# A two-layer graph network on one core: the first edge pass over windows of 32 nodes, its rows moved within SBUF

## The chip, the cores and the metric

The kernel runs on one core of one Trainium2 chip. The metric is the device time of one execution in microseconds (us). Before the change the median of three runs is 3838.8 us (3837.41 to 3846.68).

## What is computed

There are N = 3125 nodes with 128 features, E = 100,000 edges with 64 features, and for each edge a source and a destination node; the edges come sorted by destination. The first layer is, with `seg` a softmax or sum over the edges of a destination:

```python
h = node_features @ node_fc_W + node_fc_b
he = edge_features @ edge_fc_W + edge_fc_b
hs, hd = (h[src], h[dst])
a = jnp.sum(hs * hd, axis=-1)
t = jax.nn.relu(jnp.einsum('ed,mdf->emf', he, rel_att_W1) + rel_att_b1[None])
g = jax.nn.sigmoid(jnp.einsum('emf,mf->em', t, rel_att_W2) + rel_att_b2[None])
alpha = _seg_softmax(a, dst, n)
beta = _seg_softmax(g, dst, n)
s_att = jnp.einsum('ed,kdf->ef', hs, node_att_W)
h_att = jax.ops.segment_sum(alpha[:, None] * s_att, dst, num_segments=n) / kk
t_rel = jnp.einsum('ed,mdf->emf', hs, rel_att_W)
msg_rel = jnp.einsum('em,emf->ef', beta, t_rel)
h_rel = jax.ops.segment_sum(msg_rel, dst, num_segments=n) / mm
h_red = jax.nn.relu(jnp.concatenate([h_att, h_rel], axis=-1) @ out_fc_W + out_fc_b)
```

A node without edges keeps h; a gate of the node's features mixes this with the features; a layer norm follows. The second layer takes a softmax over all edges of a score `tanh(q[src] + k[dst]) @ phi`, sums messages by source, and ends in another layer norm.

## The kernel before

The program is five blocks, each with code for the five engines, joined by barriers.

**Block 1** (L327 to L912, to 683.6 us). SP loads the inputs (L330 to L356), TensorE projects the nodes in 25 blocks of BN = 125 (L470 to L486), and SP writes each block to `h_table` (rows) and `hT_table` (transposed) in DRAM (L368 to L373). ScalarE copies results out of the banks. Then comes the edge MLP in 100 "octs" of 8 x 125 edges: TensorE transposes the edge features (L526), makes six hidden products of 500 columns (L536) and six logit products (L547) that each fill 32 rows of a bank; ScalarE applies relu (L667), tanh and exp. Beside it VectorE sorts the edges by source for the second pass and makes both passes' plans: tables that say for each step which group of edges and which block of nodes it treats. At the end VectorE splits the edge weights into bf16 parts (L853 to L857) and SP writes records of ten words for each edge (L378, `rec0`).

**Block 2, the first edge pass** (L916 to L1164, 683.6 to about 2227 us). GROUPS = 196 groups of 512 edges meet NB = 25 blocks of nodes in STEPS = 220 steps; a step treats one group for one block. It is a loop of ten steps (SU); the ring of gathered rows has five slots (RING). In a step:

- SP reads group and block from the plan by two `value_load` (L969, L970) and loads the records (L972) and the block's node vectors `hbT` (L973).
- POOL gathers 4 x 128 rows of `h_table` by indirect DMAs (L984) into `hs`, two steps and more ahead.
- TensorE turns back the exponentials of step n (L1022), turns the rows (L1000) and the one-hot table (L1006) of step n + 2, makes the scores of step n + 1 (L1017), the relation sums (L1030), their weights' sums (L1033) and the attention sums (L1039) of step n.
- ScalarE copies the turned rows (L1061), makes a mask of the turned one-hot (L1063), the exponentials (L1073), and copies them turned back (L1069).
- VectorE makes the one-hot table (L1101, L1104), the maximum over scores and mask (L1126), the weighted one-hot (L1111), and adds the sums to the block's (L1140, L1143, L1145), with a running maximum and a factor `shrink` (L1075) between steps.

The order of work on each engine is written out by hand in the function `body` of each; what an engine may start is set by semaphores. TensorE's order and the slot rule of the gathers are:

```python
turn_back(s, k); turn(*step_of(s, k, 2)); scores(*step_of(s, k, 1)); relations(s, k); attention(s, k)
pool.wait_ge(stepped, s * SU + k + SU - RING + 1)
```

**Block 3** (L1170 to L1404) turns the sums into outputs (L1226 to L1237, L1361), applies gate and layer norm (L1366 to L1378), and writes the tables of keys, values and queries. **Block 4** (L1411 to L1690) is the second edge pass, 220 steps of the same kind, with gathers at L1482 and TensorE's sums at L1528. **Block 5** writes the output.

## Time and profile before

| | |
|---|---|
| median of 3 runs | 3838.8 us (3837.41 to 3846.68) |
| profiled execution | 3869.89 us |
| its span | 3868.0 us, mean granted clock 0.837 |
| TensorE (PE) busy | 2980.1 us (77%) |
| VectorE (DVE) | 2193.4 us (57%) |
| GpSimd (POOL) | 1902.0 us (49%) |
| ScalarE (ACT) | 1479.6 us (38%) |
| DMA | 231,858 packets, 217.93 MB, 161,623 of them under 512 B |

The span runs from the first to the last instruction; the execution's own time is the one to compare with the runs. Busy shares are averages over five blocks with different limits. The granted clock is the TensorE clock that was allowed, as a share of the full 2.4 GHz. PEld is TensorE's loading of weights. In the rows, `arena` is the memory that holds `hs`, the weighted one-hot and, in block 1, the hidden layers.

### The profile page before, as it was taken

The numbers are of one execution on the slowest core, as the hardware profiler recorded it, in microseconds if no ns is written. First come the engines' busy times: TensorE is split into PE (matmuls) and PEld (weight loads), VectorE is DVE, ScalarE is ACT, GpSimd is POOL, SyncE is SP. The second block draws the span as 40 slices with busy tenths as digits, with TensorE's granted clock in tenths as the row PEclk, the third lists the DMA queues.
The fourth block names the chain that finished last, engine by engine and source line by source line (L and its number), as shares of the span: only waits on it lengthen the run. The fifth ranks groups of instructions, "written<-read, shape, count | busy, mean of one in ns | idle before, by whom it ended". The sixth has DMA issues, their size and how long they took to land. (4 is left out here: it accounts for less than half of the span.)

```text
span 3868.0 us, 66746 instructions
## 1 busy us (share of the span) xinstructions
PE 2980.1 (77%) x17025; PEld 2039.3 (53%) x17025; DVE 2193.4 (57%) x5947; ACT 1479.6 (38%) x3759; POOL 1902.0 (49%) x1791
## 2 busy tenths in 40 slices
PE   5999999698989889898889936665665666656663
PEld 3444333466666666666666634554554555545552
DVE  8455210566666656666656673655555555555554
ACT  3777776233333334333333322222222222222221
POOL 0000000566666656666656502666666666666660
PEclk9999999799999989999999965776667777677675
DMA  2111121212212112222212102222222222222220
GB/s 69 57 45 45 55 76 39 60 48 52 52 49 50 50 47 52 49 52 51 49 48 50 39 2 60 72 70 70 70 71 72 70 70 71 71 71 72 71 69 19
DMA packets 231858, 217.93 MB, mean 56 GB/s; under 512 B 161623, under 2 KB 190124, under 8 KB 231787
## 3 DMA queue, kind: packets, MB, share of 16 engines
q0 software_dynamic: 70400, 144.29, 14.0%
q1 hardware_dynamic: 161387, 72.74, 7.5%
q8 instruction: 38, 0.62, 0.1%
q14 instruction: 33, 0.27, 0.0%
HBM read 203.65 MB, written 13.22 MB: 56 GB/s over the span
## 5 line engine op out<-in xcount | busy, mean ns | idle before, releaser
L984 POOL DMA_INDIRECT arena<-h_table,rec x880 | 976.4, 1110 | 545.8 <-issue 249.9
L1482 POOL DMA_INDIRECT arena<-kv_table,rec_sb x880 | 911.8, 1036 | 471.7 <-issue 235.3
L1030 PE MATMUL bank<-arena 128*128 128x375 f32 x1760 | 611.3, 490 | 0.0
L1528 PE MATMUL bank<-arena,probT 128*125 128x193 f32 x1760 | 513.8, 456 | 122.3 <-DVE probT L1646 65.6
L1528 PEld LDWEIGHTS bank<-arena,probT 128*125 128x125 f32 x1760 | 422.8, 265 | 179.7 <-DVE probT L1646 103.3
L1030 PEld LDWEIGHTS bank<-arena 128*128 128x128 f32 x1760 | 349.4, 199 | 302.0 <-issue 122.6
L1522 PE MATMUL bank<-top_run,ones 1*128 1x1 f32 x440 | 108.6, 313 | 367.8 <-DVE top_run L1625 196.4
L1111 DVE TENSOR_TENSOR arena<-onehot,rec 128x1500 f32<-128x1500 bf16 x220 | 376.5, 1711 | 0.0
L536 PE MATMUL bank<-eaT,wc 64*128 64x500 f32 x1200 | 360.8, 616 | 0.0
L1572 ACT COPY hotT<-bank 125x512 bf16<-125x512 bf16 x220 | 128.1, 582 | 580.4 <-remote 514.3
L1126 DVE CUSTOM_DVE_ANT_0 score<-bank,mask,m_old 125x512 f32<-125x512 f32 x220 | 165.2, 751 | 296.3 <-remote 178.8
L1522 PEld LDWEIGHTS bank<-top_run,ones 1*128 1x128 f32 x440 | 89.9, 253 | 453.2 <-DVE top_run L1625 243.1
L667 ACT ACTIVATE arena<-bank,bias 128x500 f32<-128x500 f32 x534 | 314.6, 684 | 36.6 <-PE bank L536 32.3
L977 POOL MEMSET arena<- 128x20 f32 x1 | 0.1, 134 | 649.5 <-POOLq L328 649.5
L1069 ACT COPY probT<-bank 128x500 f32<-128x500 f32 x220 | 126.8, 576 | 439.3 <-PE bank L1022 309.4
L1073 ACT ACTIVATE prob<-score,m_neg 125x512 f32<-125x512 f32 x220 | 158.8, 722 | 343.4 <-DVE m_neg L1129 308.6
L1022 PE MATMUL bank<-identf,prob 125*128 125x125 f32 x880 | 146.5, 292 | 165.5 <-issue 95.2
L1017 PE MATMUL bank<-hsT,hbT 128*125 128x512 f32 x440 | 272.0, 704 | 0.0
L1039 PE MATMUL bank<-arena,probT 128*125 128x129 f32 x1760 | 248.6, 283 | 0.0
L1617 DVE TENSOR_TENSOR arena<-bank,arena 128x256 f32<-128x256 f32 x220 | 92.7, 421 | 245.3 <-remote 235.9
L536 PEld LDWEIGHTS bank<-eaT,wc 64*128 64x128 f32 x1200 | 133.1, 186 | 164.1 <-ACT arena L667 105.9
L1646 DVE TENSOR_TENSOR probT<-onehot,p_e 128x500 f32<-128x500 bf16 x220 | 149.7, 680 | 115.9 <-ACT p_e L1565 80.1
(291 smaller groups left out, 4881.7 us busy)
## 6 DMA issues: line engine op xcount, KB each, us to landing
ea<-in_edge_attr SPq DMA_DIRECT2D x100, 250.0 KB
arena<-h_table,rec POOLq DMA_INDIRECT x880
arena<-kv_table,rec_sb POOLq DMA_INDIRECT x880
hbT<-hT_table SPq DMA_DIRECT2D x220, 62.5 KB
qb<-q_table SPq DMA_DIRECT2D x220, 46.9 KB
rec<-rec SPq DMA_DIRECT2D x220, 20.0 KB
rec<-rel_st SPq DMA_DIRECT2D x5, 781.2 KB
rec_sb<-rec SPq DMA_DIRECT2D x220, 4.0 KB
```

What stands on the lines that cost most here:

```text
L536: pe.matmul(bank[1 + (6 * o + n) % 4][:, 0:4 * LANES], wc[half * DE:(half + 1) * DE, m * D:(m + 1) * D], eaT[half * DE:(half + 1) * DE, o ...
L667: act.activation(hid[o % 3 * 6 + n], bank[1 + (6 * o + n) % 4][:, 0:4 * LANES], ACT.Relu, bias=bias1[:, m:m + 1]).then_inc(hid_sb, 1)
L984: pool.indirect_dma_start(out=hs[:, k % RING, j, 0:D], out_offset=None, in_=h_table, in_offset=bass.IndirectOffsetOnAxis(ap=rec_v[:, k, j, ...
L1017: pe.matmul(bank[2][0:BN, :], hbT[:, k, :], hsT[:, k % 2, :], start=True, stop=True).then_inc(score_ps, 1)
L1030: pe.matmul(bank[6 + k % 2][:, 0:M * BN], hs[:, k % RING, j, 0:D], hot_w_v[:, k % 2, j, :], start=(j == 0), stop=(j == GT - 1))
L1039: last = pe.matmul(bank[4 + k % 2][0:BN, 0:D + 1], probT_v[:, k % 2, j, :], hs[:, k % RING, j, :], start=(j == 0), stop=(j == GT - 1))
L1073: act.activation(prob[:, k % 2, :], score[:, k % 2, :], ACT.Exp, bias=m_neg[:, k % 2:k % 2 + 1]).then_inc(prob_done, 1)
L1111: v.tensor_tensor(hot_w[:, k % 2, :].rearrange("p (j m n) -> p j m n", j=GT, m=M), onehot_v[:, k % RING, :, :].unsqueeze(2).to_broadcast([ ...
L1126: v.tensor_tensor_reduce(score[:, q, :], bank[2][0:BN, :], mask[:, q, :], 1.0, m_old[:, q:q + 1], ALU.add, ALU.max, m_new[:, q:q + 1]).the ...
L1482: pool.indirect_dma_start(out=row_v[:, k % RING, j, 0:KV], out_offset=None, in_=kv_table, in_offset=bass.IndirectOffsetOnAxis(ap=rec_v[:, ...
L1522: pe.matmul(bank[3][:, 0:1], ones[0:1, :], top[0:1, k:k + 1], start=True, stop=True).then_inc(top_ps, 1)
L1528: last = pe.matmul(bank[4 + k % 2][0:BN, 0:KV + 1], probT_v[:, k % 2, j, :], row_v[:, k % RING, j, AD:RK], start=(j == 0), stop=(j == GT - 1))
```

## The change

- Node blocks have 128 rows for 125; the last has 53.
- The first pass goes over windows of WN = 32 nodes: 98 windows, STEPS0 = 296 steps in a loop of eight. Each of the four sub-groups of 128 edges of a step sums into its own 32 rows of a bank, so the accumulators `att_acc` and `rel_acc` hold four partial sums (of lanes) that block 3 merges. The sums of weights come from a column of ones in `hs`.
- POOL gathers once for each group (196 x 4 gathers, written out without a loop) into a landing ring of four groups in `y_sb`. For each step SP moves the group's 4 x 128 rows from there into a second ring `hs` of four slots by a DMA within SBUF, and reads three numbers from the plan. VectorE reads four and ScalarE one.
- The records of the first pass go: source, destination and weight stay in SBUF by group (`src_g`, `dst_g`, `w_g`). `src_g` and `dst_g` are loaded again from the inputs in pieces of 16 B, and all tables of nodes must have been written before ScalarE starts on the edge MLP.
- The MLP has 98 octs of 8 x 128 edges. The bf16 split of the weights goes, and the counting that makes the plan runs over 98 windows.
- Block 3 has a merge of the lanes' maxima and sums, a rescaling of the accumulators in five pieces, and tables written without a ring. Blocks 4 and 5 change only in size.

The diff, cut to its core:

```diff
-BN = 125
-NB = N // BN
+BN = 128
+NB = -(-N // BN)
+NP = NB * BN
+LAST = N - (NB - 1) * BN
...
+WN = 32
+WINS = -(-N // WN)
...
+STEPS0 = -(-(GROUPS + WINS - 1) // SU0) * SU0
+SH = 4
+RING0 = 4
...
-                    with sp.Fori(0, NB // W) as s:
-                        for k in range(W):
-                            b = s * W + k
-                            sp.wait_ge(hT_sb, b + 1)
-                            sp.dma_start(h_table[bass.ds(b * BN, BN), :], hblk[:, k, :]).then_inc(h_out[k], 16)
-                            sp.dma_start(hT_table[bass.ds(b, 1), :, :].rearrange("o d n -> (o d) n"), hT[:, k, :]).then_inc(h_out[k], 16)
...
+                        def load_group(table, name):
+                            sp.dma_start(table[:, 0:COLS - GT].rearrange("p (g j) -> p g j", j=GT),
+                                         i[name][0:FULL].rearrange("(g p j) -> p g j", p=128, j=GT)).then_inc(groups_in, 16)
+                            sp.dma_start(table[0:TAIL, COLS - GT:],
+                                         i[name][FULL:].rearrange("(p j) -> p j", j=GT)).then_inc(groups_in, 16)
+
+                        for o in range(U):
+                            load_edges(o)
+                        load_group(dst_g, "dst")
+                        load_group(src_g, "src")
+                        for b in range(NB):
+                            sp.wait_ge(hT_sb, b + 1)
+                            sp.dma_start(h_table[b * BN:(b + 1) * BN, :], h_sb[:, b, :]).then_inc(h_out, 16)
+                            sp.dma_start(hT_table[:, b * BN:(b + 1) * BN], hT[:, b, :]).then_inc(h_out, 16)
+                        for o in range(U, OCTS):
...
+                    act.wait_ge(h_out, 32 * NB)
...
                 def _(sp):
-                    with sp.Fori(0, STEPS // SU) as s:
-                        for k in range(SU):
-                            n = s * SU + k
-                            g = sp.value_load(plan_row[0][0:1, bass.ds(n * 2, 1)], min_val=0, max_val=GROUPS - 1)
-                            b = sp.value_load(plan_row[0][0:1, bass.ds(n * 2 + 1, 1)], min_val=0, max_val=NB - 1)
-                            sp.wait_ge(stepped, n + 1)
-                            sp.dma_start(rec[:, k, :], rec0_v[bass.ds(g, 1), :, :].rearrange("o p w -> (o p) w")).then_inc(loaded[k], 16)
-                            sp.dma_start(hbT[:, k, :], hT_table[bass.ds(b, 1), :, :].rearrange("o d n -> (o d) n")).then_inc(loaded[k], 16)
+                    sp.wait_ge(cleared_a, 1)
+                    sp.sem_inc(moved[SH - 1], 16)
+                    with sp.Fori(0, STEPS0 // SU0) as s:
+                        for k in range(SU0):
+                            n = s * SU0 + k
+                            b = sp.value_load(row0(1, n), min_val=0, max_val=WINS - 1)
+                            sp.wait_ge(stepped, n + SU0 - SH + 1)
+                            sp.dma_start(hbT[:, k % SH, :], hT_table[:, bass.ds(b * WN, WN)]).then_inc(window_in[k % SH], 16)
+                            g = sp.value_load(row0(0, n), min_val=0, max_val=GROUPS - 1)
+                            slot = sp.value_load(row0(2, n), min_val=0, max_val=RING0 - 1)
+                            sp.wait_ge(ready, g + 1)
+                            sp.dma_start(hs[:, k % SH, :, 0:D],
+                                         landed_rows[:, bass.ds(slot * GT * D, GT * D)].rearrange("p (j d) -> p j d", j=GT)).then_inc(moved[k % SH], 16)
+                            sp.wait_ge(moved[(k - 1) % SH], 16 * (SU0 // SH) * s + 16 * ((k + SH - 1) // SH) + (0 if k % SH else 16))
+                            sp.sem_inc(copied, 1)
+                    sp.wait_ge(moved[SH - 1], 16 * (STEPS0 // SH) + 16)
+                    sp.sem_inc(copied, 1)
 
                 @block.gpsimd
                 def _(pool):
-                    pool.memset(hs[:, :, :, D:D + 1], 1.0).then_inc(cleared, 1)
-                    with pool.Fori(0, STEPS // SU) as s:
-                        for k in range(SU):
-                            pool.wait_ge(loaded[k], 32 * s + 32)
-                            pool.wait_ge(stepped, s * SU + k + SU - RING + 1)
-                            pool.sem_inc(ticks, 1)
-                            for j in range(GT):
-                                pool.indirect_dma_start(
-                                    out=hs[:, k % RING, j, 0:D], out_offset=None, in_=h_table,
-                                    in_offset=bass.IndirectOffsetOnAxis(ap=rec_v[:, k, j, 0:1], axis=0)).then_inc(gathered[k % RING], 16)
+                    def gather(g, k):
+                        pool.sem_inc(ticks, 1)
+                        for j in range(GT):
+                            at = (k * GT + j) * D
+                            pool.indirect_dma_start(
+                                out=landed_rows[:, at:at + D], out_offset=None, in_=h_table,
+                                in_offset=bass.IndirectOffsetOnAxis(ap=src_g[:, g * GT + j:g * GT + j + 1], axis=0)).then_inc(landed[k], 16)
+                    for g in range(GROUPS):
+                        k = g % RING0
+                        if g >= RING0:
+                            last_step = pool.value_load(reach_row[0:1, g - RING0:g - RING0 + 1], min_val=0, max_val=STEPS0 - 1)
+                            pool.wait_ge(copied, last_step + 2)
+                        gather(g, k)
+                        if g:
+                            pool.wait_ge(landed[(g - 1) % RING0], 64 * ((g - 1) // RING0 + 1))
+                            pool.sem_inc(ready, 1)
+                        if g == RING0 - 1:
+                            pool.memset(area_b, 0.0).then_inc(cleared_b, 1)
+                    pool.wait_ge(landed[RING0 - 1], 64 * (GROUPS // RING0))
...
-                        pe.matmul(bank[2][0:BN, :], hbT[:, k, :], hsT[:, k % 2, :], start=True, stop=True).then_inc(score_ps, 1)
+                        pe.wait_ge(hot_done, n + 1)
+                        pe.wait_ge(prob_done, n + 1)
+                        pe.matmul(bank[1 + k % 2][:, 0:128], far_rows[0:1, 0, :], far_rows[0:1, 1, :], start=True, stop=False)
+                        for j in range(GT):
+                            pe.matmul(bank[1 + k % 2][j * WN:(j + 1) * WN, 0:128], onehot_v[:, k % SH, j, :], big_ident[:, :],
+                                      start=False, stop=False)
+                        for j in range(GT):
+                            last = pe.matmul(bank[1 + k % 2][j * WN:(j + 1) * WN, 0:128], hbT[:, k % SH, :], hsT[:, k % 2, j * 128:(j + 1) * 128],
+                                             start=False, stop=True)
+                        last.then_inc(score_ps, 1)
...
+                        pe.transpose(bank[3][:, 0:128], prob[:, k % 2, :], identf[:, :]).then_inc(probT_ps, 1)
...
-                            pe.matmul(bank[6 + k % 2][:, 0:M * BN], hs[:, k % RING, j, 0:D], hot_w_v[:, k % 2, j, :],
+                            pe.matmul(bank[6 + k % 2][0:M * WN, 0:D + 1], hot_w_v[:, k % SH, j, :], hs[:, k % SH, j, :],
                                       start=(j == 0), stop=(j == GT - 1))
-                        for j in range(GT):
-                            pe.matmul(bank[4 + k % 2][0:BN, 256:256 + 3 * M], onehot_v[:, k % RING, j, :],
-                                      rec_p[:, k, j, 10:10 + 3 * M], start=(j == 0), stop=(j == GT - 1))
...
-                            last = pe.matmul(bank[4 + k % 2][0:BN, 0:D + 1], probT_v[:, k % 2, j, :], hs[:, k % RING, j, :],
-                                             start=(j == 0), stop=(j == GT - 1))
+                            last = pe.matmul(bank[4 + k % 2][j * WN:(j + 1) * WN, 0:D + 1], probT[:, k % 2, j * WN:(j + 1) * WN],
+                                             hs[:, k % SH, j, :], start=True, stop=True)
...
+                    def exponentials(s, k):
+                        n, q = s * SU0 + k, k % 2
+                        b = act.value_load(row0(1, n), min_val=0, max_val=WINS - 1)
+                        act.wait_ge(max_done, n + 1)
+                        act.mul(m_neg[:, q:q + 1], m_new[:, q:q + 1], -1.0).then_inc(neg_done, 1)
+                        act.wait_ge(neg_done, n + 1)
+                        act.wait_ge(probT_ps, n + 1)
+                        act.activation(prob[:, q, :], bank[1 + q][:, 0:128], ACT.Exp, bias=m_neg[:, q:q + 1]).then_inc(prob_done, 1)
+                        act.wait_ge(summed, 2 * n + 2)
+                        act.activation(shrink[:, q:q + 1], m_st[:, bass.ds(b, 1)], ACT.Exp, bias=m_neg[:, q:q + 1]).then_inc(shrink_done, 1)
...
+                        g = v.value_load(row0(0, n), min_val=0, max_val=GROUPS - 1)
+                        v.wait_ge(score_ps, n + 1)
+                        v.tensor_scalar(gone[:, k % 2, :], dst_g[:, bass.ds(g * GT, GT)], base0[:, bass.ds(n, 1)], None,
...
                     def weigh(s, k):
 
-                        v.wait_ge(hot_done, s * SU + k + 1)
-                        v.tensor_tensor(hot_w[:, k % 2, :].rearrange("p (j m n) -> p j m n", j=GT, m=M),
-                                        onehot_v[:, k % RING, :, :].unsqueeze(2).to_broadcast([128, GT, M, BN]),
-                                        rec_w[:, k, :, 2:2 + M].unsqueeze(3).to_broadcast([128, GT, M, BN]),
+                        n = s * SU0 + k
+                        g = v.value_load(row0(0, n), min_val=0, max_val=GROUPS - 1)
+                        v.wait_ge(hot_done, n + 1)
+                        v.wait_ge(stepped, n + SU0 - SH + 1)
+                        v.tensor_tensor(hot_w[:, k % SH, :].rearrange("p (j m n) -> p j m n", j=GT, m=M),
+                                        onehot_v[:, k % SH, :, :].unsqueeze(2).to_broadcast([128, GT, M, WN]),
+                                        w_g[:, bass.ds(g * GT, GT), :].unsqueeze(3).to_broadcast([128, GT, M, WN]),
                                         ALU.mult).then_inc(hotw_done, 1)
                     def maximum(s, k):
 
-                        n, q = s * SU + k, k % 2
-                        b = v.value_load(plan_row[0][0:1, bass.ds(n * 2 + 1, 1)], min_val=0, max_val=NB - 1)
+                        n, q = s * SU0 + k, k % 2
+                        b = v.value_load(row0(1, n), min_val=0, max_val=WINS - 1)
                         v.wait_ge(m_stored, n + 1)
-                        v.tensor_scalar(m_old[:, q:q + 1], m_st[:, bass.ds(b, 1)], 1.0, None, ALU.mult).then_inc(old_read, 1)
-                        v.wait_ge(score_ps, n + 1)
-                        v.wait_ge(mask_done, n + 1)
-                        v.wait_ge(old_read, n + 1)
+                        v.wait_ge(score_ps, n + 5)
                         v.sem_inc(ticks, 1)
-                        v.tensor_tensor_reduce(score[:, q, :], bank[2][0:BN, :], mask[:, q, :], 1.0, m_old[:, q:q + 1],
-                                               ALU.add, ALU.max, m_new[:, q:q + 1]).then_inc(max_done, 1)
-                        v.wait_ge(max_done, n + 1)
-                        v.tensor_scalar(m_neg[:, q:q + 1], m_new[:, q:q + 1], -1.0, None, ALU.mult).then_inc(neg_done, 1)
-                        v.tensor_scalar(m_st[:, bass.ds(b, 1)], m_new[:, q:q + 1], 1.0, None, ALU.mult).then_inc(m_stored, 1)
+                        v.tensor_scalar(junk[:, :], bank[1 + q][:, 0:128], m_st[:, bass.ds(b, 1)], None, ALU.max, ALU.max,
+                                        accum_out=m_new[:, q:q + 1]).then_inc(max_done, 1)
...
+                    v.memset(area_a, 0.0).then_inc(cleared_a, 1)
+                    v.wait_ge(cleared_a, 2)
+                    v.wait_ge(cleared_b, 1)
```

How the instructions move. SP's queue, one step of the first pass before:

```order
L969 TENSOR_LOAD plan_row
L969 ISA x2
L970 ISA
L970 TENSOR_LOAD plan_row
L970 ISA x2
L971 REGISTER_ALU
L972 ISA
L972 DMA rec<-rec 128x40
L973 ISA
L973 DMA hbT<-hT_table 128x125
```

And after, from the window's load on (a plan read stands ahead of it):

```order
L965 ISA
L965 DMA hbT<-hT_table 128x32
L966 ISA
L966 TENSOR_LOAD plan_row
L966 ISA x2
L967 ISA
L967 TENSOR_LOAD plan_row
L967 ISA x2
L968 REGISTER_ALU
L969 ISA
L969 DMA hs<-y_sb 128x4x128
L971 ISA
```

Two reads and two loads from DRAM became three reads, one load and the move; the last row is the count that releases POOL.

SP's queue in block 1, before, from the last small load to the first two table writes:

```order
L356 DMA next_i<-in_dst 124x1
L359 DMA rec<-pad 88x40
L368 UNCONDITIONAL_BRANCH
L368 ISA
L372 ISA
L372 DMA h_table<-hblk 125x128
L373 ISA
L373 DMA hT_table<-hT 128x125
```

And after:

```order
L361 DMA next_i<-in_dst 124x1
L370 DMA rel_acc<-in_edge_attr 128x2x256 x4
L377 DMA dst_g<-in_dst 128x195x4
L379 DMA dst_g<-in_dst 40x4
L377 DMA src_g<-in_src 128x195x4
L379 DMA src_g<-in_src 40x4
L388 DMA h_table<-h_sb 128x128
L389 DMA hT_table<-att_acc 128x128
```

The loads of edge features and of the groups now stand between the small loads and the table writes.

VectorE's queue in a step of the first pass, from the maximum to the weighted one-hot, before:

```order
L1119 ISA
L1119 TENSOR_LOAD plan_row
L1119 ISA x2
L1120 REGISTER_ALU
L1121 ISA
L1121 TENSOR_SCALAR m_old<-m_st 125x1
L1126 ISA score,m_new<-bank,mask,m_old 125x512
L1126 ISA m_new 125x1
L1129 TENSOR_SCALAR m_neg<-m_new 125x1
L1130 TENSOR_SCALAR m_st<-m_new 125x1
L1111 TENSOR_TENSOR arena<-onehot,rec 128x1500
```

And after:

```order
L1140 ISA
L1140 TENSOR_LOAD plan_row
L1140 ISA x2
L1142 REGISTER_ALU
L1144 ISA
L1144 TENSOR_SCALAR junk,m_new<-bank,m_st 128x128
L1129 TENSOR_LOAD plan_row
L1129 ISA x2
L1131 REGISTER_ALU
L1132 ISA
L1132 TENSOR_TENSOR hot_w<-onehot,w_g 128x384
```

The maximum lost its two small companions and has 128 columns for 512; the weighted one-hot has 384 columns for 1500, and a plan read of its own.

## Rows read from the trace of the kernel before

**Rows 1.** Stages: stretch, length, busy of each engine with instructions, PEclk, DMA share, GB/s.
```profile
92.00:683.00 591.00, 570.16 (x2978) 231.02 (x2977) 194.44 (x349) 419.80 (x760) 0.00 (x0) 0.99 0.17 54
...
704.00:2227.00 1523.00, 1354.06 (x7463) 971.83 (x7462) 973.84 (x2416) 578.68 (x1102) 964.73 (x869) 0.93 0.20 50
2227.00:2386.00 159.00, 90.67 (x400) 64.84 (x400) 94.56 (x305) 41.20 (x151) 1.47 (x2) 0.61 0.08 23
2386.00:3788.00 1402.00, 880.14 (x5940) 721.24 (x5940) 805.74 (x2640) 397.18 (x1541) 914.58 (x882) 0.71 0.27 70
```

**Rows 2.** Timeline of TensorE, a quiet step: start, us, engine, line, op, tiles, count.
```profile
1223.96 0.59 PE L1022 MATMUL bank<-identf,prob 125*128 125x125 f32 x4
1224.38 0.60 PE L1000 MATMUL bank<-identf,arena 128*128 128x128 f32 x4
1224.82 0.39 PE L1006 MATMUL bank<-identb,onehot 128*125 128x128 bf16 x4
1225.05 1.07 PE L1017 MATMUL bank<-hsT,hbT 128*125 128x512 f32 x2
1225.96 2.69 PE L1030 MATMUL bank<-arena 128*128 128x375 f32 x8
...
1228.69 1.13 PE L1039 MATMUL bank<-arena,probT 128*125 128x129 f32 x8
...
1229.66 0.59 PE L1022 MATMUL bank<-identf,prob 125*128 125x125 f32 x4
```

**Rows 3.** Timeline of a late step: in brackets the idle time before, and its releaser.
```profile
1202.17 1.07 PE L1017 MATMUL bank<-hsT,hbT 128*125 128x512 f32 x2
...
1208.84 0.69 ACT L1063 ACTIVATE mask<-bank,neg_big 125x512 f32<-125x512 bf16 x1 [1.53 <-remote]
1209.06 0.75 DVE L1126 CUSTOM_DVE_ANT_0 score<-bank,mask,m_old 125x512 f32<-125x512 f32 x1 [4.90 <-remote]
```

**Rows 4.** Timeline of POOL, one gather of 128 rows.
```profile
691.68 0.95 POOL L984 DMA_INDIRECT arena<-h_table,rec  x1 [0.31 <-issue]
```

**Rows 5.** Timeline of SP's queue, first edge pass.
```profile
688.93 0.33 SPq L973 DMA_DIRECT2D hbT<-hT_table  x1
690.84 0.34 SPq L972 DMA_DIRECT2D rec<-rec  x1
691.37 0.33 SPq L973 DMA_DIRECT2D hbT<-hT_table  x1
```

**Rows 6.** Timeline of TensorE in the MLP: first hidden product, and grouped products.
```profile
102.83 4.47 PE L536 MATMUL bank<-eaT,wc 64*128 64x500 f32 x12
...
322.29 2.72 PE L547 MATMUL bank<-arena,w_shift 128*32 128x500 f32 x24
324.95 0.65 PE L526 MATMUL bank<-identf,ea 125*128 125x125 f32 x4
```

**Rows 7.** DMA busy tenths in 40 slices of 686.2 to 687.9 us.
```profile
DMA  0000000147642131000003169995333211000007
```

**Rows 8.** DMA packets of 28.4 to 30.8 us.
```profile
DMA packets 1015, 0.24 MB, mean 100 GB/s; under 512 B 550, under 2 KB 1015, under 8 KB 1015
```

**Rows 9.** Timeline of SP's queue, loads of the start.
```profile
12.81 0.30 SPq L351 DMA_DIRECT2D x_sb<-in_x  x1
13.15 15.59 SPq L353 DMA_DIRECT2D w<-in_L_gnn_rel_att_W  x1
```

**Rows 10.** Groups of POOL, 2227 to 2500 us: total us, mean ns, idle.
```profile
L1474 POOL MEMSET rel_st<- 125x4825 f32 x1 | 4.1, 4126 | 0.0
```

**Rows 11.** Timeline, end of the MLP and start of the pass.
```profile
672.21 0.59 DVE L853 CAST rel_st<-rel_st 125x480 bf16<-125x480 f32 x1 [99.72 <-ACT rel_st L681]
...
675.40 0.27 SPq L378 DMA_DIRECT2D rec<-rel_st  x1
...
683.60 0.13 POOL L977 MEMSET arena<- 128x20 f32 x1 [649.50 <-POOLq L328]
```

**Rows 12.** Timeline of VectorE, one wide operation of layer norm 1.
```profile
2305.18 3.49 DVE L1377 TENSOR_TENSOR y_sb<-y_sb,mean 125x3200 f32<-125x3200 f32 x1
```

1150 lines of the change are left out of this document (570 added, 580 removed).

## The prediction

> **What bounds the kernel now.** I read the busy time by stage first, then one step of each pass as a timeline, then the issuing queues (SP, POOL), then the transfers. The stage table [rows 1] splits the 3868.0 us of the span into the edge MLP and its table (92 to 683), the first edge pass (704 to 2227, 1523 us), the stage between the passes (159 us) and the second pass (1402 us). The change rewrites the first pass, so the question is what ends last there. TensorE is busy 1354 of 1523 us at a granted clock of 0.93. A quiet step [rows 2] has TensorE work end to end: from one turn-back (L1022) at 1223.96 to the next at 1229.66, 5.70 us, of which the relation sums (L1030, four matrix products of 375 columns, two records each) take 2.69 and the attention sums (L1039) 1.13. So 5.70 us is TensorE's own work. But 1523 / 220 steps = 6.92 us: some steps are late by more. In one of them [rows 3] TensorE's scores (L1017) end at 1203.24 in the records, while ScalarE's mask waits till 1208.84 and VectorE's maximum till 1209.06 (4.90 us idle, put down to "remote"). These late arrivals cost 1.2 us a step on average. POOL's gathers, 4 x (0.95 + 0.30) us [rows 4], would allow 5.0 us a step, and SP 2.44 us a step (688.93 to 691.37, [rows 5]): neither sets the pass.
>
> **The first pass after the change.** There are 296 steps for 220; each sums into 32 nodes and not 125.
>
> TensorE, at the durations of [rows 2]: turn-back falls from four transposes to one, 0.15; turn stays 0.60; the four bf16 transposes of L1006 go, and five bf16 products of 128 columns come (0.10 each by L1006): 0.5; the scores are four products of 128 columns in separate 32-row groups. Such groups exist today in L547, 12 products of 500 columns (24 records) in 2.72 us [rows 6], 0.23 each where one of 512 columns in L1017 takes 1.07, so they run about four at a time: 0.27. Relations, four of 129 columns, 1.13 like L1039; attention, four of 129 in groups, 0.28. Sum 2.9 us for 5.7. TensorE alone would thus give 296 x 2.9 = 860 us at the full clock; it will not set the step, and something else must. The Trainium skill (TensorEngine Tiling (Array Packing), Key Properties) says that changing the tiling mode drains TensorE, which speaks against four mode changes a step; in [rows 6] the transposes after the grouped products start at 324.95, before the modelled end of the last of these at 325.01, so this trace shows no such cost.
>
> POOL: 784 gathers x 1.25 us / 296 = 3.3 us a step. VectorE: its datapath work falls (the 1500-element product becomes 384 elements), but it now reads four numbers from the plan in a step and not two. A read costs about 0.79 us: on SP two of them fill the gap from 689.26 (688.93 + 0.33) to 690.84 [rows 5]. Four of them are 3.2 us, and with its other instructions I estimate 4.1 us: a floor. SP: three reads and two DMAs, 2.4 + 1.1 = 3.5 us.
>
> The new path is the move. SP may start the move into a slot of the ring of four only when the attention of four steps before is done, and TensorE turns rows two steps ahead; so one round of this loop must fit into two steps. The round: issue of the window's DMA, two plan reads, issue of the move, 0.33 + 0.2 + 1.58 + 0.33 + 0.2 = 2.64 us [rows 5]; the move itself; then turn, scores, relations, attention on TensorE, 2.8 us at full clock; semaphores 0.2. The move is not in this trace. It has 512 pieces of 512 B. Nearest row: 128 pieces of 500 B, issued at 686.12, in flight in the 21st to the 34th of the 40 slices of 0.0425 us of [rows 7], that is from 0.9 us after the issue and for 0.6 us; so 512 pieces take 0.9 + 2.4 = 3.3 us. Bounds: 0.9 + 512 / 423 = 2.1 us at the piece rate of [rows 8], and 0.9 + 512 / 200 = 3.5 us at the rate of the load of x (3,125 pieces, behind which SP's next DMA is held for 15.59 us, [rows 9]). I take 3.3, the row with the same kind of piece. Then 2T = 2.64 + 3.3 + 2.8 + 0.2 = 8.9, T = 4.5 us. The Trainium skill (DMA: Bandwidth & Descriptors, Anatomy of one DMA) fits a DMA at 2.0 us plus its bytes at 436 GB/s, which for 262,144 B is an estimated 2.6 us and would give T = 4.1; no transfer within SBUF is in this trace.
>
> The clock: in the second pass TensorE is busy 880 of 1402 us and gets 0.71 [rows 1]. With 2.9 us of work in a step the first pass comes into the same state, 2.8 us becomes 3.7 and T = 4.9 us. And if late arrivals cost 1.2 us as they do today, with half of the clock's loss, 4.7 + 1.2 = 5.9. I take the middle of 4.5 and 5.9, **5.2 us**: the late arrivals are in the one gather pass read here step by step, but I don't know their cause and the new step has a slack of two steps to absorb them.
>
> Start of the pass: 16 gathers (20 us), then POOL's memset of 12,900 elements, 11.0 us by 4126 ns for 4825 [rows 10], on which VectorE's first step waits; with the first transfers and waits 36 us. Pass: 36 + 296 x 5.2 = 1575 us against 2227 - 683.6 = 1543 (from POOL's first instruction [rows 11] to the end of the stretch in [rows 1]): **+32 us**.
>
> **Stage 1.** Sources and destinations of the edges are loaded again by group: 49,920 pieces of 16 B on SP's queues, issued ahead of the node tables' writes, and ScalarE now waits for all table writes before its first copy of the MLP. Behind this wait stand TensorE and the whole MLP, which is bound by TensorE (570 of 591 us, [rows 1]), so a delay counts in full. SP is through with the large loads at about 30 us today [rows 9]. Rate of small pieces: 1015 packets in 2.4 us, 423 per us, half of them under 512 B [rows 8], which gives 118 us. At the 200 per us of [rows 9] it would be 250 us; at the other end nearly nothing, if the pieces don't travel as such. I take 118, the row that has small pieces in it. Then 6,400 pieces of the tables' writes at 128 in 0.6 us: 30 us. The first hidden product starts at 30 + 118 + 30 = 178 us for 102.83 [rows 6]: +75. The MLP itself has 98 x 512 columns for 100 x 500: +2. At its end VectorE's splits (from 672.21) and the record store (issued 675.40), ahead of the next stage at 683.60 [rows 11], go: -10. **+67 us.** The other edits here (one counting of 98 windows for 25 of blocks, later turns of the sort) lie on VectorE, which is busy 194 of 591 us: nothing.
>
> **Stage between the passes.** Four lanes of sums are merged, all sums rescaled by ten operations of 2,560 elements (2.8 us each by 3.49 us for 3,200 [rows 12]), four of them ahead of the first block (11 us), a merge chain of some ten small operations (8 us) ahead of that; I take the blocks' products to cost what they cost now. Less one copy a block and the ring of the tables: **+15** (between -10 and +30). **Second pass**: blocks of 128 for 125, 0.5% of 1402: **+7**.
>
> **Sum**: 32 + 67 + 15 + 7 = +121 on the profiled execution's 3869.9 us. The profiled execution is 0.8% over the median of the runs, 3838.8; on that, **3960 us**. A difference of 0.3% is about what a measurement of this kernel can tell from none.
>
> **Rivals.**
> - *The step falls to VectorE's or the move's floor, and the kernel is faster.* If the move runs at the piece rate of rows 8 (2T = 7.7) VectorE's 4.1 us sets the step, and with little lateness T = 4.35: the pass takes 36 + 296 x 4.35 = 1324 us, -219, in sum -130: 3709 us. The kernel breaks even when the pass takes 1543 - 89 = 1454 us, T = 4.79. For it: TensorE has half the work, and two steps of slack swallow a late result. Against it: the lateness and clock of [rows 1, 3]. 33%.
> - *The moves collide with the gathers.* The moves carry 256 KB a step as the gathers do, in 512 pieces more. If lateness stays in full and the clock falls, T = 5.9: pass 1782, +239, in sum 4167 us. 20%.
> - *The small pieces are hidden* (merged, or moved beside x): stage 1 gives -8 and not +67, the rest as forecast: 3885 us. 8%.
> - Break-even within 0.3%: 5%. My forecast (T of 4.85 to 5.5 with stage 1 delayed): 34%.
>
> Faster 33%, same 5%, slower 62%. The range takes in most of the first rival and of the second: 3690 to 4150 (the far halves of the tails of both, some 2 in 10, lie outside).
>
> **What would show it.** After: first hidden product near 178 us, preceded by a ScalarE wait on the table writes; 49,920 packets under 512 B before it. In the first pass a step of 5.2 us, TensorE idle before the turn and waiting for a move; moves of some 3.3 us from issue; a granted clock near 0.7. Wrong if TensorE never waits for a move (then T is set by plan reads or exponentials), if T is under 4.79, or if the hidden products start before 110 us.

## The result, and the profile after

The changed kernel takes 4141.66 us (median of four runs, 4135.07 to 4165.76), the kernel before 3842.74 us (median of four, 3837.41 to 3848.26): 1.0789 times as long, 95% interval 1.0741 to 1.0837. The direction was forecast and the range held the median by 8 us, but the difference is +299 us where +121 was forecast. The profiled execution has a span of 4142.6 us for 3868.0, +274.6.

The experiments below fell on several machines, and one and the same kernel differs between them by up to 15% (before) and 19% (after). "Machine" means the chip on which a set of runs fell. Each set of experiments fell on another one, at a time of its own, so chip and time can't be told apart. Times are compared within a set unless it is said otherwise.

The stages of the changed kernel; the rows answer to [rows 1] (stretch, length, busy of PE, PEld, DVE, ACT, POOL, granted clock, DMA share, GB/s):

```profile
84.00:669.00 585.00, 563.27 (x2899) 222.26 (x2898) 250.48 (x480) 418.34 (x755) 0.00 (x0) 0.99 0.15 44
...
704.00:2447.00 1743.00, 1173.19 (x10043) 784.69 (x10043) 589.75 (x2067) 527.99 (x1774) 734.88 (x766) 0.71 0.27 76
2447.00:2673.00 226.00, 162.70 (x679) 139.33 (x679) 102.76 (x242) 33.08 (x106) 4.04 (x2) 0.50 0.06 17
2673.00:4060.00 1387.00, 897.82 (x5907) 724.36 (x5908) 806.46 (x2622) 393.13 (x1530) 898.98 (x882) 0.69 0.27 71
```

The balance, stage by stage:

| stage | before | after | difference | forecast |
|---|---|---|---|---|
| block 1 (to POOL's first instruction of the pass) | 683.6 | 669.8 | -14 | +67 |
| first edge pass (to 2227 and 2447) | 1543 | 1777 | +234 | +32 |
| between the passes | 159 | 226 | +67 | +15 |
| second edge pass | 1402 | 1387 | -15 | +7 |
| end | 80 | 83 | +3 | 0 |

Block 1. SP's queue and TensorE's first hidden product (answer to [rows 6, 9]), and POOL's first gather (answer to [rows 11]):

```profile
24.91 0.47 SPq L377 DMA_DIRECT2D dst_g<-in_dst  x1
25.42 16.85 SPq L379 DMA_DIRECT2D dst_g<-in_dst  x1
42.31 0.38 SPq L377 DMA_DIRECT2D src_g<-in_src  x1
42.74 13.71 SPq L379 DMA_DIRECT2D src_g<-in_src  x1
...
84.11 2.87 PE L551 MATMUL bank<-rel_acc,wc 64*128 64x512 f32 x6
...
669.76 1.18 POOL L982 DMA_INDIRECT y_sb<-h_table,src_g  x1 [643.86 <-issue]
```

The 24,960 pieces of 16 B of the first table hold SP for 16.85 us: 1480 per us, not 423. SP is through with both tables at 56 us, and the MLP starts at 84.11, earlier than the 102.83 of before. The node stage starts earlier (TensorE's first product at 25.23 us for 33.32) and takes 1.77 us a block for some 2.3; it has no ring any more.

The first pass. Two waits of the changed kernel between 760 and 2400 us (engine, line, releaser: us in total, times, longest), and a late step (answer to [rows 3]), with the first and the last of the four gathers that POOL does meanwhile:

```profile
DVE junk L1144 <- remote: 416.4, 138, 8.7
...
PE bank L1036 <- ACT prob L1084: 363.7, 197, 8.1
```

```profile
1503.98 0.94 POOL L982 DMA_INDIRECT y_sb<-h_table,src_g  x1 [3.13 <-SPq L972]
...
1506.05 0.39 PE L1027 MATMUL bank<-hsT,hbT 128*32 128x128 f32 x8
...
1507.78 0.94 POOL L982 DMA_INDIRECT y_sb<-h_table,src_g  x1 [0.30 <-issue]
...
1510.11 0.35 DVE L1144 TENSOR_SCALAR_CACHE_REDUCE junk<-bank,m_st 128x128 f32<-128x128 f32 x1 [3.45 <-remote]
1510.50 0.20 ACT L1081 ACTIVATE m_neg<-m_new 128x1 f32<-128x1 f32 x1 [3.91 <-DVE junk L1144]
```

From the first turn-back at 706.13 to the 296th at 2445.06 a step takes 5.89 us (median 5.15), 83 of them over 7 us. The scores end at 1506.44 in the records and VectorE sees them at 1510.11; ScalarE waits for VectorE, and TensorE for ScalarE. Such a result, seen by the others some us after its recorded end, is called a late arrival below.

Between the passes, one block of the changed kernel (TensorE):

```profile
2530.76 1.75 PE L1257 MATMUL bank<-lane_sel,att_acc 128*128 128x32 f32 x8
2532.33 0.88 PE L1259 MATMUL bank<-identf,rel_acc 96*128 96x96 f32 x4
2533.00 1.97 PE L1270 MATMUL bank<-w_fold,sumT 128*128 128x128 f32 x8
2534.76 1.54 PE L1257 MATMUL bank<-lane_sel,att_acc 128*128 128x32 f32 x7
```

A block takes 4.0 us (2530.76 to 2534.76), at a clock of 0.50, and the 25 blocks 100.4 us (2460.3 to 2560.7). I had priced it at what it cost before. There the 25 blocks took 35.9 us (2227.2 to 2263.0), 1.4 us each, at a clock of 0.95:

```profile
2227.00:2263.00 36.00, 29.08 (x225) 26.64 (x225) 25.39 (x89) 22.96 (x75) 0.00 (x0) 0.95 0.00 1
```

### The profile page after: what moved, and what is told of

Its sections match the earlier page's. It is cut to its first block and busy times, and to the rows that moved or that the text cites. A ratio compares the mean times of both kernels' runs of the same rounds, so it can differ in the third digit from the quotient of the medians.

```text
span 4142.6 us, 81962 instructions
## 1 busy us (share of the span) xinstructions
PE 2888.0 (70%) x19840; PEld 1932.1 (47%) x19840; DVE 1869.6 (45%) x5647; ACT 1414.1 (34%) x4343; POOL 1673.7 (40%) x1700
## 5 line engine op out<-in xcount | busy, mean ns | idle before, releaser
L982 POOL DMA_INDIRECT y_sb<-h_table,src_g x784 | 752.9, 960 | 1616.9 <-issue 851.6
L1509 POOL DMA_INDIRECT att_acc<-kv_table,rec_sb x880 | 898.8, 1021 | 485.7 <-issue 241.5
L1555 PE MATMUL bank<-att_acc,probT 128*128 128x193 f32 x1760 | 534.5, 470 | 108.0 <-DVE probT L1673 72.6
L1555 PEld LDWEIGHTS bank<-att_acc,probT 128*128 128x128 f32 x1760 | 439.5, 277 | 171.9 <-DVE probT L1673 125.1
L1043 PE MATMUL bank<-hs,hot_w 128*96 128x129 f32 x2368 | 501.4, 378 | 4.0 <-issue 4.0
L1043 PEld LDWEIGHTS bank<-hs,hot_w 128*96 128x96 f32 x2368 | 414.1, 234 | 93.7 <-issue 81.3
L672 ACT ACTIVATE att_acc<-bank,bias 128x512 f32<-128x512 f32 x588 | 350.4, 694 | 37.8 <-PE bank L551 33.3
L551 PE MATMUL bank<-rel_acc,wc 64*128 64x512 f32 x1176 | 360.4, 628 | 0.2 <-ACT att_acc L672 0.2
L1012 PE MATMUL bank<-identf,hs 128*128 128x128 f32 x1184 | 255.7, 356 | 124.5 <-DMA hs<-y_sb 122.5
L1012 PEld LDWEIGHTS bank<-identf,hs 128*128 128x128 f32 x1184 | 179.6, 184 | 154.7 <-issue 150.7
## 6 DMA issues: line engine op xcount, KB each, us to landing
hs<-y_sb SPq DMA_DIRECT2D x296, 256.0 KB
rel_acc<-in_edge_attr SPq DMA_DIRECT2D x97, 256.0 KB, 2.6
```

Of the source, the lines that this page charges most:

```text
L551: pe.matmul(bank[1 + (6 * o + n) % 4][:, :], wc[half * DE:(half + 1) * DE, m * D:(m + 1) * D], eaT[half * DE:(half + 1) * DE, o % 3, :], s ...
L672: act.activation(hid[o % 3 * 6 + n], bank[1 + (6 * o + n) % 4][:, :], ACT.Relu, bias=bias1[:, m:m + 1]).then_inc(hid_sb, 1)
L982: pool.indirect_dma_start(out=landed_rows[:, at:at + D], out_offset=None, in_=h_table, in_offset=bass.IndirectOffsetOnAxis(ap=src_g[:, g * ...
L1012: last = pe.transpose(bank[0][:, j * 128:(j + 1) * 128], hs[:, k % SH, j, 0:D], identf[:, :])
L1043: pe.matmul(bank[6 + k % 2][0:M * WN, 0:D + 1], hot_w_v[:, k % SH, j, :], hs[:, k % SH, j, :], start=(j == 0), stop=(j == GT - 1))
L1509: pool.indirect_dma_start(out=row_v[:, k % RING, j, 0:KV], out_offset=None, in_=kv_table, in_offset=bass.IndirectOffsetOnAxis(ap=rec_v[:, ...
```

## The experiments

The first theories were: A, the gathers make the late arrivals; B1, the loop of the move sets the step; C, the chain from scores over maximum and exponentials to the turn-back sets it, with or without the clock. The table has what all runs gave; the step is the mean from the first to the last turn-back of the first pass, "over 7" the number of steps longer than 7 us, "before" the kernel before on the same machine.

| run | time | before | step | over 7 | first step of pass 2 less last of pass 1 |
|---|---|---|---|---|---|
| before, recorded | 3842.7 | | 6.91 | 91 | 181 |
| after, recorded | 4141.7 | 3842.7 | 5.89 | 83 | 238 |
| few_gathers | 3528.4 | 3388.9 | 4.54 | 0 | 238 |
| small_move | 3470.9 | 3388.9 | 4.35 | 0 | 238 |
| early_reads | 3513.3 | 3388.9 | 4.49 | 0 | 238 |
| warm_pe | 3748.8 | 3388.9 | 5.29 | 1 | 241 |
| after_again | 3529.5 | 3390.4 | 4.55 | 0 | 238 |
| before_again | 3383.6 | 3390.4 | 5.71 | 1 | 181 |
| shared_g | 3375.1 | 3390.4 | 4.02 | 0 | 238 |
| early_gb | 3339.2 | 3390.4 | 3.93 | 0 | 239 |
| gb_ring8 | 4205.4 | 3887.9 | 5.96 | 61 | 239 |
| gb_between | 4198.3 | 3887.9 | 6.03 | 73 | 227 |
| after_third | 4199.0 | 3887.9 | 5.99 | 83 | 238 |
| few_gathers_2, _3, _4 | 3525.4, 3525.7, 3526.5 | 3386 | 4.54 | 0 | 238 |
| few_small, few_small_3 | 3465.0, 3464.1 | 3386 | 4.33 | 0 | 238 |
| before_few | 3385.9 | 3386.1 | 5.71 | 1 | 180 |
| combined | 3294.9 | 3385.9 | 3.85 | 0 | 211 |

**First set: four suspects.** Fewer gathers:

```diff
-                        for j in range(GT):
+                        for j in range(GT if g < RING0 else 1):
```

> The changed kernel; after the first four groups POOL gathers only the first 128 of a group's 512 rows (the other rows of the landing ring keep old data; this leaves out three quarters of the gathered rows of the first pass). The changed kernel's first pass takes 296 steps of 5.89 us on average, a quarter of the steps over 7 us. Theory A (late arrivals are made by the gathers on POOL and their transfers): steps over 7 us mostly vanish, mean step 5.0 us or less, pass about -260 us. Theory B (late arrivals come from the moves or from TensorE's own clock changes): mean step stays within 0.2 us of 5.89, pass -60 to 0 us.

A smaller move:

```diff
-                            sp.dma_start(hs[:, k % SH, :, 0:D], landed_rows[:, bass.ds(slot * GT * D, GT * D)]...)
+                            sp.dma_start(hs[:, k % SH, 0, 0:D], landed_rows[:, bass.ds(slot * GT * D, D)])
```

> The changed kernel; each step moves only the first 128 of 512 rows (64 KB for 256), the other rows of the ring hold ones (leaves out three quarters of the move). Theory B1 (the move is the step's loop): TensorE's waits for the move (99.9 us) go, and the mean step falls from 5.89 to about 5.0 us, pass -250 us. Theory A (gathers) or C (the clock and the chain scores, maximum, exponentials, turn-back): mean step stays above 5.6 us, pass at most -90 us.

SP's plan reads first (the reads of `g`, `slot` and `b` all stand ahead of `sp.wait_ge(stepped, ...)`):

> The changed kernel with SP's three plan reads ahead of its wait for the attention of four steps before, so that 1.6 us leave the path of the move. Theory B1 (the move's loop of two steps sets the step): T falls by up to 0.8 us, pass -150 to -240 us. Theory C (the chain from scores through maximum and exponentials to turn-back sets it, 364 us of TensorE's waits): -30 to -100 us, only TensorE's waits for the move go.

More work on TensorE:

```diff
                             attention(s, k)
+                            for r in range(4):
+                                pe.matmul(bank[3][:, 128:512], identf[:, :], x_sb[:, 0:3, :]..., start=True, stop=True)
```

> The changed kernel with four more matrix products of 384 columns on TensorE after each step's attention, results unused: 1.3 us more work in a step at full clock. Theory C1 (the clock of 0.71 is what makes the step long): the granted clock of the pass rises above 0.85 and the mean step stays at 5.9 us or falls, despite the work. Theory A or B: the clock may rise, but the step gets longer by 0.5 to 1.3 us, pass +150 to +390 us.

All four fell on a machine on which the kernel before takes 3388.9 us and not 3842.7, and none has the late arrivals. So the set told nothing about their cause, only that they don't come on every machine. Warm_pe is the one that stands by itself: the clock of the pass is 1.00 and the step 5.29, nearly every one alike, with TensorE busy all the time:

```profile
710.00:2260.00 1550.00, 1550.00 (x12309) 996.44 (x12309) 583.72 (x2051) 525.55 (x1758) 731.90 (x762) 1.00 0.32 85
```

My price for the added work was wrong: an f32 product is two records of 0.32 us at 384 columns, so four are 2.6 us and not 1.3. TensorE's own step is then 5.29 - 2.6 = 2.7 us (2.9 was forecast).

**Second set: both kernels on such a machine, and VectorE's plan reads.**

> The changed kernel as it is. In the first set of runs the kernel before took 3388.9 us, 450 us less than in the recorded runs, and none of its variants of the changed kernel had steps over 7 us, so the late arrivals are not a property of the code alone. Theory D (the machine adds them to either kernel in some runs): here, if the kernel before is near 3389 us, the changed kernel's step is 4.6 to 4.8 us without steps over 7 us and its time is 3540 to 3600 us, still slower than before. Theory A or B (the change makes them, or makes more of them): its step stays at 5.9 us.

> The kernel before as it is, for its profile beside that of the changed kernel. Theory D: where its time is near 3389 us, the first pass has a step of 5.70 us throughout (220 steps, 1254 us) and the second one of 5.3 us, and steps over 7 us are gone; where it is near 3840 us the steps are those of the first profile.

VectorE reads the group once:

```diff
-                        g = v.value_load(row0(0, n), min_val=0, max_val=GROUPS - 1)
+                        g = kept["g"]
                         v.wait_ge(hot_done, n + 1)
```

> The changed kernel; VectorE reads the group once and not twice in a step (three plan reads for four). Theory E (VectorE's sequence of plan reads is the floor of the step, 4.1 us): step falls by 0.4 to 0.8 us against the changed kernel in the same set, pass -120 to -240 us. Theory B1 (the move's loop): step unchanged within 0.1 us.

With that, SP's reads first, and the window's number kept:

```diff
-                        b = v.value_load(row0(1, n), min_val=0, max_val=WINS - 1)
+                        b = kept[k] if k >= 2 else v.value_load(row0(1, n), min_val=0, max_val=WINS - 1)
                         v.wait_ge(stepped, n + SU0 + 1)
```

> The changed kernel with SP's three plan reads ahead of its wait, VectorE's group read once, and the window's number kept from the maximum to the sums two steps later in six of eight steps (2.25 plan reads a step for 4). Theory E with B1: step 3.6 to 4.0 us where no late arrivals are, pass -180 to -300 us against the changed kernel, so that it would be about level with the kernel before or faster. Theory C (the chain scores, maximum, exponentials, turn-back sets the step): 4.2 to 4.4 us.

Theory D holds: the changed kernel is 1.0414 (1.0395 to 1.0432) times before here, +139 us. Its step of 4.55 us and its 3529.5 us are just under what was expected (4.6 to 4.8, 3540 to 3600). The first pass of before_again and after_again, from the stage view:

```profile
704.00:1967.00 1263.00, 1256.56 (x7469) 915.38 (x7469) 984.21 (x2421) 565.26 (x1110) 974.79 (x869) 1.00 0.24 60
```

```profile
704.00:2046.00 1342.00, 1012.42 (x10000) 686.86 (x9996) 589.54 (x2061) 528.06 (x1764) 742.15 (x766) 0.82 0.37 98
```

Before is TensorE end to end, at the full clock. After, VectorE's waits of after_again (760 to 2000 us) name no engine: "issue" is time in which it waits for nothing that the profile shows, that is for its own sequence of plan reads and register instructions.

```profile
DVE junk L1144 <- issue: 199.5, 241, 1.2
DVE hot_w L1132 <- issue: 144.0, 221, 1.0
DVE att_acc L1155 <- issue: 140.5, 253, 1.0
```

Taking one of four reads away (shared_g) takes 0.53 us off the step and 154 us off the time. Against the 4.55 us here the first set's variants, from another machine without late arrivals, gain little: SP's earlier reads alone (early_reads) 0.06 us, few_gathers nothing (4.54), the smaller move 0.20 us. So theory E stands and B1 falls as the main bound. With SP's reads first, the group read once and the window's number kept (early_gb) the kernel is 1.5% faster than before: 0.985 (0.9833 to 0.9868). The step of 3.93 us is in the expected 3.6 to 4.0; first to last turn-back is 184 us shorter than in after_again (180 to 300 expected), the whole kernel 190 us.

**Third set: the next bound, and the stage between the passes.** A ring of eight:

```diff
-SH = 4
+SH = 8
+HR = 4
...
-            hot_w = sb2("hot_w0", [128, SH, GT * M * WN])
+            hot_w = sb2("hot_w0", [128, HR, GT * M * WN])
```

> early_gb with a ring of eight slots for the moved rows and the one-hot tables (four for the weighted one-hot), so that SP may move four steps earlier. Theory B1 as the next bound (in early_gb TensorE waits 147 us for moves in 1090 us, and 108 us for the exponentials): the waits for moves go and the step falls from 3.93 to 3.5 to 3.8 us, -40 to -130 us. If the chain of scores, maximum, exponentials and turn-back is the next bound: within 20 us of early_gb.

Two products of 384 columns more in each block between the passes (in `outs`, into bank 5):

> early_gb with two more matrix products of 384 columns in each block's outputs between the passes, results unused. There the changed kernel has TensorE and its weight loads busy all the time at a granted clock of 0.50, 4.0 us a block. Theory F (the half clock makes this stage long): the clock rises towards 1.0 and a block takes 2.0 us for its own work plus 1.3 us for the added, 3.3 us, stage -10 to -20 us in spite of the added work. Theory G (the work itself, not the clock): the clock stays at 0.50 and a block gets 2.6 us longer, stage +60 us.

> The changed kernel once more. Theory D (late arrivals come with the machine on which a run falls): if the kernel before is near 3390 us in this set, the step is 4.5 to 4.6 us and the time 3520 to 3540 us; if it is near 3840 us, the step is 5.9 us and the time 4130 to 4170 us.

This set fell on a machine with late arrivals (3887.9 us for before). There, after_third has its 5.99 us a step again (its 4199 us are over the 4170 expected, as the kernel before is over 3840), and gb_ring8 (5.96) and gb_between (6.03, in the pass the same code as early_gb) have it too: what took 0.6 us off the step on the other machine gains nothing here. VectorE's time has only changed its name, from its own sequence to late results (gb_ring8, 760 to 2400 us):

```profile
DVE junk L1146 <- remote: 541.9, 116, 9.1
```

Ring depth can't be judged on this machine, and neither of the two expectations of gb_ring8 applies. Between the passes theory F holds. The stage view of gb_between and of after_third:

```profile
2500.00:2560.00 60.00, 59.62 (x395) 50.73 (x396) 24.84 (x13) 10.99 (x34) 0.00 (x0) 0.92 0.00 1
```

```profile
2480.00:2560.00 80.00, 72.41 (x361) 72.16 (x362) 31.95 (x19) 11.63 (x36) 0.00 (x0) 0.50 0.00 1
```

In after_third the weight loads are busy 72.16 of 72.41 us in which TensorE is: blocks of many loads and few columns, at the half clock. Loads that fill the engine don't tell the clock by themselves, though: in the kernel before they were busy 26.64 of 29.08 us in these blocks, at 0.95. With 768 columns more in a block the clock is 0.92 and the block, added work and all, takes 3.4 us for 4.0; the stage is 11 us shorter (238 to 227).

**Fourth and fifth set: the gathers once more.** before_few is the kernel before with `for j in range(1)` in POOL's loop; few_small is few_gathers and small_move together.

> The changed kernel with a quarter of the gathers of the first pass again (leaves out three quarters of the gathered rows). Where the kernel before takes about 3390 us: step 4.5 us as in the first set. Where it takes about 3840 to 3890 us, the late arrivals are there, and this tells what makes them: theory A (the gathers): steps over 7 us mostly go, mean 4.5 to 4.8 us; theory H (something that the gathers don't touch, as the loop or the engines' own signals): mean stays 5.9 to 6.0 us.

> A quarter of the gathers and a quarter of each move (leaves out three quarters of both). At about 3390 us for before: step 4.3 us. At 3840 us or more: theory A' (all transfers together make the late arrivals): mean 4.3 to 4.5 us and none over 7 us, even if few_gathers_2 keeps some; theory H: 5.8 to 6.0 us.

> The kernel before with only the first of the four gathers in each step of the first pass (leaves out three quarters of the gathered rows). At about 3390 us for before: step 5.70 us, no change, since TensorE bounds it. At 3840 us or more: theory A: step 5.7 to 5.9 us for 6.91, pass -230 to -270 us; theory H: 6.7 to 6.9 us.

> The changed kernel with a quarter of the gathers of the first pass, a third time, since the two sets before fell on machines without late arrivals (3389 and 3386 us for the kernel before). Where before takes 3840 us or more: theory A (the gathers make the late arrivals): no steps over 7 us, mean 4.5 to 4.8 us; theory H (not the gathers): 5.9 to 6.0 us. Otherwise 4.54 us as twice before.

> A quarter of the gathers and of each move again. Where before takes 3840 us or more: theory A': mean 4.3 to 4.5 us; theory H: 5.8 to 6.0 us. Otherwise 4.3 us as in the set before.

All five fell on machines without late arrivals (3386 us for before). They show only that without them the gathers bound neither kernel (4.54 us, 5.71 us), and that all transfers together are worth 0.22 us a step (4.33).

**Last set.** gb_ring8 with one product of 384 columns in each block between the passes, and few_gathers a fourth time:

> gb_ring8 with one added matrix product of 384 columns in each block between the passes. Where before takes about 3390 us: early_gb was 3339; the waits for moves (147 us in 1090) shrink with the deeper ring, step 3.5 to 3.8 us for 3.93, and a block between the passes takes 2.7 to 3.4 us for 4.0: 3220 to 3310 us, 2 to 5% under before. Where before takes 3840 us or more: the step stays near 5.96 us and only the blocks gain, 4160 to 4200 us.

> A quarter of the gathers once more. Where before takes 3840 us or more: theory A: step 4.5 to 4.8 us; theory H: 5.9 to 6.0 us. Otherwise 4.54 us as three times before.

Again a machine without late arrivals. combined takes 3294.9 us, 0.9726 (0.971 to 0.9742) of before. Its blocks between the passes take 2.74 us at a clock of 0.96 (forecast 2.7 to 3.4):

```profile
1901.60 0.97 PE L1259 MATMUL bank<-lane_sel,att_acc 128*128 128x32 f32 x8
1902.41 0.53 PE L1261 MATMUL bank<-identf,rel_acc 96*128 96x96 f32 x4
1902.78 1.08 PE L1272 MATMUL bank<-w_fold,sumT 128*128 128x128 f32 x8
1903.70 0.81 PE L1275 MATMUL bank<-x_sb,identf 128*128 128x384 f32 x2
1904.34 0.97 PE L1259 MATMUL bank<-lane_sel,att_acc 128*128 128x32 f32 x8
```

The step is 3.85 us, not the 3.5 to 3.8 expected of the deeper ring: TensorE still waits for moves. SP's queue shows why:

```profile
1405.98 0.34 SPq L968 DMA_DIRECT2D hbT<-hT_table  x1
1406.54 0.64 SPq L970 DMA_DIRECT2D hs<-y_sb  x1
1409.74 0.34 SPq L968 DMA_DIRECT2D hbT<-hT_table  x1
1410.30 0.64 SPq L970 DMA_DIRECT2D hs<-y_sb  x1
```

3.76 us from move to move, and the view of waits has none for SP from 760 to 1800 us: three plan reads and two DMAs fill its queue. Nine in ten of combined's moves are 3.75 us or more after the one before, half of them 3.85 or more. The queue is the bound now (3.5 us had been estimated for it), and nearly so in early_gb already, where SP waits 7.5 us in 1040 and the moves are 3.87 us apart (median). That fewer reads on SP would lift it was not tried.

**What the traces say of the late arrivals.** No run leaves the gathers out on a machine that has late arrivals, but five profiles from such machines hold the answer to when they come. A trace has the time of a semaphore's update beside the recorded end of the instruction that makes it. In the changed kernel the updates of VectorE and ScalarE come 0.01 us behind; TensorE's are up to 8.9 us behind in after and 9.7 in gb_ring8. I count one as late over 0.8 us, and sort the first pass by whether the product ended during a burst of POOL's gathers (gathers at most 0.6 us apart), within 1.2 us after one, or outside (the updates that the traces hold, from 60 us behind the first gather to the last one):

| run | late during a burst | within 1.2 us after | outside |
|---|---|---|---|
| before | 350 of 710 | 6 of 132 | 0 of 73 |
| after | 351 of 503 | 41 of 96 | 0 of 411 |
| after_third | 305 of 470 | 45 of 104 | 0 of 424 |
| gb_ring8 | 361 of 543 | 18 of 52 | 0 of 416 |
| gb_between | 351 of 504 | 19 of 52 | 0 of 446 |
| after_again | 0 of 721 | 0 of 129 | 0 of 240 |

In the second pass 2 of 390 outside are late in the same five profiles, 2717 of 3649 during a burst.

The late step shown above fits: POOL gathers from 1503.98 to 1508.72, the scores end in between, and VectorE sees them 1.4 us after the burst. When the last gather is done, at 2406.5 us in after, the pass goes on for ten steps, with the same code, its plan reads and seven more moves, and from 1.2 us later nothing is late. There a step takes 4.0 us, as in after_third (4.1) and after_again (4.1); gb_ring8 has 3.4 there for combined's 3.5, and gb_between 3.6 for early_gb's 3.5. VectorE's waits of after from 2410 us on name no "remote" any more, and the clock is 0.89:

```profile
2410.00:2446.00 36.00, 28.44 (x307) 19.61 (x306) 16.94 (x61) 15.44 (x53) 0.00 (x0) 0.89 0.20 54
```

So theory H (the loop, the engines' own signals) doesn't fit, nor do the moves, and theory A fits: late arrivals come while POOL gathers or just after, with 2 exceptions in 2160. That is a coincidence in time, read from five profiles, and not a run in which the cause was taken away. It also doesn't say what in a gather does it (POOL's instructions or the transfers), and after_again shows that gathers alone don't make late arrivals.

## Why the prediction was right or wrong

The sign was right and the range held the time; the size was not right (+299 us for +121). The step that failed is the one that lets the first pass absorb the late arrivals, and two more terms are mis-sized, one of them the other way.

- **The step of 5.2 us, the middle of 4.5 and 5.9** (term +32, measured +234). This is the term that decided. In the recorded profile the step is 5.89 us: the number of the second rival, T = 5.9, +239 us, with a clock of 0.71 and the late arrivals in full. Its reason, that the moves collide with the gathers, isn't borne out: before has no moves and has late arrivals, and with moves and no gathers there are none. The "slack of two steps to absorb them" absorbed nothing: between machines with and without them before lost 6.91 - 5.71 = 1.20 us a step, the changed kernel 5.89 - 4.55 = 1.34, the fall of its clock from 0.82 to 0.71 included. Over the steps that is 296 x 1.34 - 220 x 1.20 = 133 us of the pass's difference, the larger part, 91 of them for the 76 steps more; 106 us are there without late arrivals (POOL's first instruction to the last turn-back: 1379 us for 1273). It isn't a fixed price of a step, though: the code of early_gb goes from 3.93 to 6.03 us (gb_between), 2.10 us more. With late arrivals every variant of the new pass takes 5.9 to 6.0 us a step, however short its quiet step is.
- **What goes with the late arrivals stood in the view of [rows 3].** I wrote "I don't know their cause" beside a late step through which POOL gathers: its last gather before VectorE's maximum ends at 1207.72 us, the mask starts at 1208.84 and the maximum at 1209.06.

```profile
1198.69 0.95 POOL L984 DMA_INDIRECT arena<-h_table,rec  x1 [0.30 <-issue]
...
1206.77 0.95 POOL L984 DMA_INDIRECT arena<-h_table,rec  x1 [0.30 <-issue]
```

- **What sets a quiet step.** I took the loop of the move (2T = 8.9, T = 4.5, or 4.9 at the lower clock) and kept VectorE's 4.1 us as a floor under it. Without late arrivals the step is 4.55 us, but for the other reason: VectorE's reads (shared_g -0.53 us), hardly the move (early_reads -0.06, small_move -0.20). A tenth of the steps are at 4.14 us or less, near the floor of 4.1 us. Beside it VectorE waits 132.6 us for TensorE in the 1240 us from 760 to 2000 us of after_again (67.4 + 31.2 + 23.4 + 10.6), 0.49 us a step, which is about the rest. That 4.5 came out was luck: the right number from the wrong loop would have led to the wrong repair.
- **The move**, 3.3 us forecast. In few_gathers, where it stands alone, it lands 2.7 us after its issue (the DMA view gives `256.0 KB, 2.7`). The estimate of 2.6 us from the Trainium skill (DMA: Bandwidth & Descriptors, Anatomy of one DMA), which the page fits to DMAs issued by GpSimd and which I had set against a row of another kind of transfer, was the better one. My row was also read a slice too early: the 128 pieces are in flight in the 22nd to the 34th slice, 0.55 us. The move's 512 pieces are in flight for 1.1 us (view of 1500 to 1505 us), over 460 per us and not 213. It isn't the path.
- **The small pieces of block 1** (term +67, measured -14). The rate of [rows 8] was that of a few small DMAs between large pieces; one large DMA of 16-byte pieces goes at 1480 per us. With that rate the sum would have been 34 + 30 us after the other loads, and all of it beside the node stage. With the measured -14 in its place the forecast would have been +40, further off: this error hid part of the one in the step. By the prediction's own sign (hidden products before 110 us; 84.11 was measured) it was wrong here.
- **The stage between the passes** (term +15, measured +67, outside its -10 to +30). "I take the blocks' products to cost what they cost now" failed: 1.4 us a block became 4.0, 65 us in 25 blocks. gb_between and combined show that most of it is the clock (3.4 and 2.74 us with more work). In combined the added product takes 0.64 of the 2.74 us (1903.70 to 1904.34), so I estimate the block's own work at 2.1 us near full clock: about 48 us are the clock and 18 us the larger work.
- **The second pass** (+7, measured -15): blocks of 128 cost next to nothing. Without late arrivals its step is 5.30 us for 5.28; the -15 is a difference between two profiles with late arrivals.
- **The rivals.** The first (T = 4.35, faster) fell for the recorded machine, and its condition, little lateness, is met elsewhere: there T = 4.55, and with the terms above the kernel is still slower, 1.0414. The break-even of T = 4.79 was computed with the stage terms that failed. That small pieces are hidden was right, and had 8%.
- **The near hit elsewhere is chance.** On the machine of the second set the difference is +139 us, close to +121, but from other terms. The profiled spans differ by 146 us: +106 for the pass (32 forecast), +57 from its last turn-back to the second pass (15), -4 from there on (7) and -13 in block 1 (67).

**What stays open** is why some machines have late arrivals and others don't, and by what way POOL's gathers hold up TensorE's results there. It isn't the code of the change, as both kernels have them on the same machines and neither elsewhere; VectorE's reads and the depth of the ring change nothing in it. That they come only with gathers is read from the traces; the runs that leave gathers out all met machines without late arrivals. In the MLP, which has no gathers, the updates of after are at most 0.05 us behind.

## What to carry to other kernels

Count the plan reads of every engine as work: at some 0.8 us each on SP's queue, and 0.53 us of the step for one on VectorE's, they set the floor of a short step where busy time shows an engine half idle. Reading a number once and keeping it was worth 154 us here, on a machine without late arrivals, and nothing was gained by it on one with them. When a trace has waits that end late without a reason, look at what every other engine does meanwhile before averaging them into a price per step: here POOL's gathers stood beside them in the same view. And take the clock of a stage from a row of like work, not from its busy share: the blocks between the passes ran at 0.95 before and at 0.50 after, TensorE's loads being busy most of the time in both.
